# A selective scan in a whole-network kernel: the residual moved to PE, one drive copy moved ahead, forward weights prepared first

## What is computed

```
def _mamba(x, in_w, conv_w, conv_b, xproj_w, dt_w, dt_b, Alog, Dp, out_w):
    xz = x @ in_w.T
    xi, z = jnp.split(xz, 2, axis=-1)
    xc = conv(xi, conv_w)                       # 4 taps, causal, per channel
    u = silu(xc + conv_b)
    x_dbl = u @ xproj_w.T                       # dt (8), B (16), C (16)
    delta = softplus(dt @ dt_w.T + dt_b)
    dA = exp(delta * A);  dBu = delta * B * u   # A = -exp(Alog)
    h = dA * h + dBu                            # for each of 16 states, along the sequence
    y = sum_n(h * C) + u * Dp
    return y * silu(z) @ out_w.T

out_fw = _mamba(x, fw_...) + x
out_bw = flip(_mamba(flip(x), bw_...) + flip(x))
out = concat([out_fw, out_bw]) @ proj_w.T + proj_b    # then a layer norm
```

## Time and profile before

| | us |
|---|---|
| median of 3 runs (4114.66 to 4116.60) | 4115.82 |
| the profiled execution, own time | 4115.49 |
| its span in the trace | 4113.7 |
| scan stage, preparation to last copy | about 2261 to 3270 |
| PE busy, whole span | 3329.7 (81%) |
| VectorE busy | 2554.8 (62%) |
| ScalarE busy | 1835.2 (45%) |
| GpSimd busy | 1192.8 (29%) |

### The profile page before, as it was taken

How to read it: one execution, slowest core, us unless ns; L and a number is a source line. 1 busy time by engine, 2 the same in 40 slices (tenths; PEclk the granted TensorE clock), 3 DMA queues, 4 the chain that set the end, 5 groups by cost and what they waited for, 6 DMA issues and landing times. The chain is left out here.

```text
span 4113.7 us, 47520 instructions
## 1 busy us (share of the span) xinstructions
PE 3329.7 (81%) x12501; PEld 1552.5 (38%) x12573; DVE 2554.8 (62%) x3976; ACT 1835.2 (45%) x2839; POOL 1192.8 (29%) x1006
## 2 busy tenths in 40 slices
PE   5599986999996498877798688878888768569998
PEld 2122225444443254433444233333333344444443
DVE  6888864333345477745433699999999743544444
ACT  2166652444435255534233576777677423202221
POOL 3211110000002222200000599999999600100000
PEclk7699996999997699979799799999999869769999
DMA  4522110000004633110000343333334110000000
GB/s 138 130 61 60 59 45 0 0 0 0 0 26 113 161 98 86 55 31 0 0 0 1 125 155 134 144 144 144 134 144 144 72 39 2 0 0 0 0 0 20
DMA packets 131062, 253.69 MB, mean 62 GB/s; under 512 B 24773, under 2 KB 100954, under 8 KB 113434
## 3 DMA queue, kind: packets, MB, share of 16 engines
q1 hardware_dynamic: 126842, 250.55, 18.8%
q0 software_dynamic: 4096, 1.59, 0.2%
HBM read 191.98 MB, written 56.89 MB: 60 GB/s over the span
## 5 line engine op out<-in xcount | busy, mean ns | idle before, releaser
L941 DVE TENSOR_REDUCE a_top<-a_sc 128x1 f32<-128x512 f32 (+3 forms) x1024 | 545.1, 585 | 166.9 <-PE a_sc L818 95.4
L1846 DVE TENSOR_TENSOR_SCAN a_g<-a_decay,a_drive 128x512 f32<-128x512 f32 x512 | 588.1, 1202 | 34.3 <-ACT a_drive L1766 34.3
L1909 POOL TENSOR_TENSOR a_g<-a_g,a_spread 128x1024 f32<-128x1024 f32 x256 | 599.5, 2359 | 27.8 <-DVE a_g L1846 27.8
L899 ACT ACTIVATE a_prob<-a_st 128x1024 f32<-128x1024 f32 (+2 forms) x512 | 419.1, 862 | 322.8 <-PE a_st L835 205.8
L1626 PE MATMUL a_y<-a_g,ident 128*128 128x512 f32 x1024 | 494.5, 624 | 55.4 <-POOL a_g L1909 50.9
L455 DVE TENSOR_TENSOR f_s<-f_a,f_spread 128x512 f32<-128x512 f32 x392 | 268.0, 688 | 434.0 <-ACT f_a L440 268.6
L422 PE MATMUL f_y<-f_s,f_w 128*128 128x512 f32 x784 | 401.3, 598 | 21.3 <-DVE f_s L455 20.7
L415 PE MATMUL f_hid<-h,f_w 128*128 x784 | 403.7, 600 | 6.0 <-PEq L246 6.0
L815 PE MATMUL a_sc<-a_k,a_q 96*128 96x512 bf16 (+3 forms) x1024 | 308.5, 357 | 41.6 <-DMA a_k<-a_k_rows 39.3
L1750 ACT ACTIVATE a_decay<-a_delta,a_capped_a 128x512 f32<-128x512 f32 x512 | 331.7, 709 | 6.5 <-DVE a_g L1846 5.9
L1626 PEld LDWEIGHTS a_y<-a_g,ident 128*128 128x128 f32 x1024 | 201.1, 201 | 342.6 <-issue 248.0
(11 more groups left out here) (330 smaller groups left out, 4910.0 us busy)
## 6 DMA issues: line engine op xcount, KB each, us to landing
a_spread<-a_bc_rows SPq DMA_DIRECT2D x128, 1024.0 KB, 4.6
a_q<-a_q_rows SPq DMA_DIRECT2D x64, 288.0 KB
a_pv_rows<-a_pv_sb SPq DMA_DIRECT2D x64, 256.0 KB, 2.1
a_q_rows<-p_qp SPq DMA_DIRECT2D x72, 128.0 KB
a_q_rows<-a1q_qp SPq DMA_DIRECT2D x72, 128.0 KB
a_k_rows<-a1q_kp SPq DMA_DIRECT2D x72, 128.0 KB
a_k<-a_k_rows SPq DMA_DIRECT2D x32, 288.0 KB
a_k_rows<-p_kp SPq DMA_DIRECT2D x72, 64.0 KB
```

The lines of the kernel that those rows point to most:

```text
L899: nc.scalar.activation(prob[w % 2][:, j, 0:width(kp)], st[:, j % 2, 0:width(kp)], ACT.Exp, scale=a.scale).then_inc(s.exp_done, 1)
L941: nc.vector.tensor_reduce(top[:, t, n:n + 1], sc[:, slot(4 * n + t) % 3, 0:w], AX.X, ALU.max).then_inc(s.maxed, 1)
L1846: nc.vector.tensor_tensor_scan(g[:, n % 8, k, way], decay[:, n % 4, k, way], drive[:, k, way], 0.0, ALU.mult, ALU.add).then_inc(scanned, 1)
L1909: nc.gpsimd.tensor_tensor(g[:, n % 8, :, :], g[:, n % 8, :, :], spread[:, pair % 4, 2 + n % 2:3 + n % 2, :].to_broadcast([P, H2, L]), ALU. ...
```

## The change

Three things, all in `layer2_mamba`:

1. The residual. `pe_out` gets a third matmul, identity times the chunk of `S.h`, into the same sum. ScalarE copies the sum into `a_o` (`act_o`), at n = 15 behind `a_du`; VectorE's add is gone. The last call of PE's `pe_out` waits for the copy before.
2. The table `COPY_AT` puts state 8's drive copy at place 7 instead of 8. At place 7 it stands ahead of the copy of the projections.
3. The loads have a semaphore for each direction. VectorE prepares the forward weights as soon as the first three transfers are there, and the first block ends. The backward weights are prepared at the start of the second block; ScalarE's exponential of the backward `Alog` stands behind the first softplus, and VectorE's negation behind the first delta. PE waits for the backward weights ahead of its first backward convolution.

```
-    COPY_AT = {3: 2, 5: 4, 8: 8, 11: 11, 14: 13, 15: 15}
+    COPY_AT = {3: 2, 5: 4, 7: 8, 11: 11, 14: 13, 15: 15}
...
+        loaded = [sem(f"a2_loaded{d}") for d in range(2)]
...
-                    dve.wait_ge(loaded, 8 * 16)
+                    dve.wait_ge(loaded[0], 3 * 16)
+                    limit(0)
+                    scale_weights(0)
+                    dve.wait_ge(prepared, 1)
+                    nc.vector.tensor_scalar(neg_a[0][:, :], neg_a[0][:, :], -1.0, None, ALU.mult)
...
-            def pe_out(U, d):
+            def pe_out(b, U, d):
                 nc.tensor.wait_ge(gated_done, U + 1)
                 for k in range(H2):
                     lo = cols["out"][0] + k * D
-                    last = nc.tensor.matmul(bank[:, 0, :], pack[d][:, lo:lo + D], gated[:, k, :],
-                                            start=(k == 0), stop=(k == H2 - 1))
-                last.then_inc(o_summed, 1)
+                    nc.tensor.matmul(bank[:, 0, :], pack[d][:, lo:lo + D], gated[:, k, :], start=(k == 0), stop=False)
+                nc.tensor.matmul(bank[:, 0, :], S.ident[:, :], h_of(b), start=False, stop=True).then_inc(o_summed, 1)
...
+            def act_o(b, d, U):
+                nc.scalar.wait_ge(o_summed, U + 1)
+                wait(nc.scalar, p_summed, b)
+                nc.scalar.activation(o[:, d, :], bank[:, 0, :], ACT.Copy).then_inc(o_done, 1)
...
                     if n == STATES - 1:
                         act_du(U + 1)
+                        if not first:
+                            act_o(b if d == 1 else b - 1, nd, U - 1)
...
-            def dve_o(b, d, U):
-                nc.vector.wait_ge(o_summed, U + 1)
-                wait(nc.vector, p_summed, b)
-                nc.vector.tensor_tensor(o[:, d, :], bank[:, 0, :], h_of(b), ALU.add).then_inc(o_done, 1)
...
                 pe.wait_ge(dve_step, 1)
+                pe.wait_ge(loaded[1], 5 * 16)
+                pe.wait_ge(prepared_1, 1)
                 pe_conv(0, 1, 1)
...
                 act_soft(0, 0)
+                act.wait_ge(limited, 2)
+                nc.scalar.activation(neg_a[1][:, :], w(1, "Alog"), ACT.Exp).then_inc(prepared, 1)
...
             def _(dve):
+                dve.wait_ge(loaded[1], 5 * 16)
+                limit(1)
+                scale_weights(1).then_inc(prepared_1, 1)
                 for q in range(len(LOG1P)):
                     dve_factor(0, 0, q)
                 dve_delta(0, 0)
+                dve.wait_ge(prepared, 2)
+                nc.vector.tensor_scalar(neg_a[1][:, :], neg_a[1][:, :], -1.0, None, ALU.mult).then_inc(prepared_1, 1)
```

More of the change, by code:

```diff
@@ L1518, in layer2_mamba @@
         proj, small = sb("proj", [P, H2, D]), sb("small", [P, 3])
-        loaded, prepared, stepped, limited = (sem(f"a2_{n}") for n in ("loaded", "prepared", "stepped", "limited"))
+        loaded = [sem(f"a2_loaded{d}") for d in range(2)]
+        prepared, stepped, limited = (sem(f"a2_{n}") for n in ("prepared", "stepped", "limited"))
         with ExitStack() as inner:
@@ L1560, in _ @@
                 def _(sp):
[L1561 to L1568 removed]
+                    loads(sp, 0, inp["a2_fw_packT"], inp["a2_fw_convT"], inp["a2_fw_dtT"])
+                    loads(sp, 1, inp["a2_bw_packT"], inp["a2_bw_convT"], inp["a2_bw_dtT"])
+                    sp.dma_start(proj[:, :, :].rearrange("p k c -> p (k c)"), inp["a2_projT"]).then_inc(loaded[1], 16)
+                    sp.dma_start(small[:, :], inp["a2_smallT"]).then_inc(loaded[1], 16)
                 @block.vector
@@ L1786, in act_unit @@
                     if last_unit:
+                        if n == STATES - 1:
+                            act_o(b, 0, U - 1)
                         continue
@@ L1866, in dve_unit @@
                         dve_gated(U - 1, nd)
-                    if n == STATES - 1 and not first:
-                        dve_o(b if d == 1 else b - 1, nd, U - 1)
                     if last_unit:
```

49 lines of the change are left out of this document (23 added, 26 removed).

## The result

| | before | after |
|---|---|---|
| median, us (9 runs each) | 4115.82 | 4127.69 |
| lowest to highest | 4111.23 to 4121.11 | 4124.94 to 4133.23 |
| profiled execution, and its span | 4115.49, 4113.7 | 4125.14, 4123.3 |

The ratio is 1.0032, with a 95% interval of 1.0023 to 1.0041. The changed kernel is slower by 13.2 us (9.5 to 16.9). The prediction said 4123.5 us, in a range of 4110 to 4132.

A forecast was written before the change was run, and what follows sets the result against it. No engine had over 4 us a unit to gain; PE ended one stretch of each unit, ScalarE's row the other. 6.9 + 0.8 + 4.3 - 4.2 = +7.8 us gave 4123.5 us, range 4110 to 4132.

The forecast's parts named there:

- Part 1, forward entries: Residual on PE, seven entries into forward units: y 0.86 us later, VectorE 0.67 earlier, so 7 x 0.25 us longer.
- Part 1, backward entries: Residual on PE, six entries into backward units: VectorE already waits for PE, so 6 x 0.86 us longer.
- Part 1, VectorE's saved add: VectorE loses one 0.67 us add a unit; into backward units that was to be only more waiting.
- F to S: Stretch from a unit's first softplus factor to state 3's scan in the next; PE ends it: 38.62 us backward, 36.81 forward.
- Part 1 as a whole: Residual on PE, copy on ScalarE: +6.9 us over the unit entries and +0.8 us after the last scan.
- S to F: Stretch from state 3's scan to the next first softplus factor; ScalarE's work ends it: 23.26 us forward, 20.79 backward.
- Part 2: Drive 8 ahead of the projections' copy: VectorE's wait moves to the first factor, 6 x 0.97 - 9 x 0.17 = +4.3 us.
- I take 0: PE's clock before the z matmuls: net effect taken as 0, ends +7.8 us (all six fall) and -11.7 (nine spared).
- Part 3: Forward weights loaded and prepared first at the start of the stage: -4.2 us (-2.5 to -5.5).
- Rival 1: PE's clock falls before z in every unit: +7.8 us more, 4131 us; chance 0.22.
- Rival 2: The added matmul costs nothing on the path, or PE's extra work spares the clock: 4112 us (4108 to 4118); chance 0.18.
- Rival 3: State 8's wait goes and does not return at the first factor: some 40 us less, 4075 to 4085; chance 0.05.

The follow-up runs named there:

- e4_no_matmul: The changed kernel without the identity matmul, so the residual is missing from the output: 0.9980 of the kernel before, stage 882.72 us.
- e2_resid: The kernel before with only the residual moved to PE and the copy to ScalarE: 4136.17 us, 1.0047 of the kernel before.
- e1_drive8: The kernel before with only state 8's drive copy moved to place 7: 0.9997 of the kernel before.
- e9_fill_after: The changed kernel with three matmuls of zeros in PE's wait ahead of z: 4119.41 us, 1.0012 of the kernel before.
- e5_conv: The changed kernel with half a convolution moved on PE from place 15 to place 3 of the next unit: 4104.97 us, 0.9978 of before.
- e12_fill_out_after: The changed kernel with three matmuls of zeros in PE's wait ahead of the output matmuls: 4113.55 us, 0.9993 of the kernel before.
- e11_full: The kernel before with one 512-column matmul of zeros added behind each unit's output matmuls: 1.0040 of the kernel before.
- e7_front_silu: The kernel before with forward weights first and the next unit's silu one place earlier on ScalarE: 4090.86 us, 0.9945 of the kernel before.
- e13_silu_fill_out: The kernel before with forward weights first, silu one place earlier, and three zero matmuls ahead of the output matmuls: 4085.31 us, 0.9925 of before.
- e10_quarter: The kernel before with one 128-column matmul of zeros added behind each unit's output matmuls: 0.9999 of the kernel before.

## Why the prediction was right, and where its steps were wrong

The sign and the time were right: slower, 4127.69 us in the range, 4.2 us over the forecast. The waits moved to the places named, with one size off: the drive's wait fell to 6.7 us and not to under 4, the first factor's rose to 48.5 (some 40 forecast), the gating's to 34.1 (some 30), with waits in forward units. But the terms of the sum were off in both directions.

- **Part 1, forward entries: mis-sized.** 7 x 0.25 was forecast, and the trace has +5.6. The term took y as 0.86 us later. It came 1.50 later. In the forward entries before, the output matmuls took 3.41 us after 3.81 of idle and the clock was at its full level behind them; in the changed kernel they take the full 3.78 after 5.87, and the residual behind them 1.34. The argument that the matmuls behind it take up the clock earlier or later by the same time, so that 0.86 is right and 1.9 only an end, is the step that failed here: the idle time ahead of the block had grown too. The sum went by the row of a backward entry for both; a forward entry before reads:

```profile
2655.49 3.41 PE L1637 MATMUL a_bank<-a_gated,a_pack 128*128 128x512 f32 x4 [3.81 <-DVE a_delta L1814]
```

- **Part 1, backward entries: right.** 6 x 0.86 = 5.2 forecast, 4.9 measured; in the late units y is 0.98 later. Here the argument held: the residual takes 1.50 us and the sum behind it 0.36 less than before, since the clock now rises ahead of them.
- **Part 1, VectorE's saved add: right.** It is only more waiting. In e4_no_matmul, with the add gone and no matmul in its place, the stage stands within 0.4 us of before.
- **Part 1 as a whole: mis-sized.** It is worth +19.3 us (e2_resid) where 6.9 + 0.8 was forecast. F to S was only half of it. The other half is the lengthened S to F, which e2_resid has with drive 8 left where it was.
- **Part 2: right in mechanism, wrong in sum.** The copy is 2.0 us later and the first factor waits for it, as forecast, but alone the move is worth -1.2 us (-5.8 to 2.9), where I had +4.3. What failed is the "I take 0" for the clock. The z matmuls went from 3.78 and 1.98 to 3.54 and 3.14 in e1_drive8, the sum behind them changed with them, and the pair came back to its 119.5. The end of that term (all nine slow ones spared) was wide enough.
- **Part 3: right, a little small.** -4.2 forecast; -5.4 in the trace and -6.2 (-10.7 to -1.6) alone. The forward weights landed 5.9 us after the start of the stage, against an estimate of 2267.0 - 2261.03 = 6.0. The rest of the difference is the first convolution, which took 9.18 us in place of 9.94. The 0.3 us that the forecast added because every restart is at half clock went the other way, and its reason does not hold: z in backward units restarts after 3.50 us of idle and runs in 1.98.
- **Rival 1** gave the pair that came: over 122.3 us, where the forecast's own was 121. Its mechanism is half there. z in backward units went from 1.98 to 2.86 us, not to 3.78, and the forward entries' output matmuls fell to half clock as well. Of the two marks that I had set, "z at 3.78 in all units and a pair over 122.3", the second came without the first.
- **Rival 2** needed PE to hold the clock because it has more work. Only matmuls that stand in the idle time did that (e9_fill_after and e5_conv for z, e12_fill_out_after for the output). One behind the block did the opposite (e11_full).
- **Rival 3** did not happen. The wait came back at the first factor in full (e1_drive8), and falls only when ScalarE's chain starts earlier (e7_front_silu).

The total came near because -6.2 and -1.2 stood beside +19.3, where the forecast had -4.2, +4.3 and +7.7. That the errors of part 1 and part 2 had different signs was luck.

## What to carry to other kernels

A small operation put on an engine that ends a repeating unit costs what it does to the unit's rhythm, not its own length: here 0.86 us of TensorE work cost 1.7 us a unit, and 0.2 us of it cost nothing. Price it in the block where it lands, at the clock of that block, and look first at the idle time ahead of that block. Here work moved into PE's idle time (a convolution half, even matmuls of zeros) brought more than the operation that one wanted to save. A wait removed from one engine is gone only when the chain that it waited for starts earlier.

## What the runs showed of the hardware

- **The pair of units has preferred lengths.** It is 119.44 to 119.5 us in five kernels and 122.88 in three, 3.4 us apart. No kernel settled between the two; the pairs of e9_fill_after and e12_fill_out_after, which fill idle time with zeros, range over 2.7 us. After a disturbance the lengths run to one of them over some six pairs, and the z times run with them (e1_drive8: z in backward units 2.54, 2.92, 3.06, 3.11, 3.14, and the pair 120.21, 119.84, 119.61, 119.52, 119.49). In these eight the granted clock repeats with the pair, as the windows above show. That the clock also holds the pair at its length would explain this, but was argued and not shown: no run changed the clock by itself. Not every steady pair needs it: e13_silu_fill_out runs at 116.45 to 116.51 us while its stretches at the lower level move from pair to pair.
- **The Trainium skill** (TensorE: Matmul & The Clock Gate, Part 1) says that the check of activity runs free of the kernel. The trace agrees in part: the same 3.50 us of idle stood ahead of z matmuls of 3.78 us (e11_full, forward), 3.40 (e10_quarter, forward), 2.86 (after, backward) and 1.98 (before, backward). But within one of the settled kernels the times didn't scatter. They went to fixed values.
- **Zeros in the idle time.** Three matmuls of zeros a unit brought the output matmuls from 3.78 to 1.98 us in 9 of 14 units, and the stage of the changed kernel from 902.57 to 886.39. With the earlier silu (e13_silu_fill_out) it was all 14.
- **Unchanged code moves too.** The start of this stage, with the same code ahead of it, stood at 2251.9 to 2266.2 us in the profiled executions of these kernels. So a few microseconds in the total say little, and the stage read between two of its own rows says more: in it e11_full and the changed kernel agree within 0.6 us.
